# Two transformer layers on one core: last batch in token halves, mask rows inside the products, and new tables of times

## The reference

```python
x = x + LN(attn0(LN(x)))     # 16 heads of 16, biases, rope, causal softmax, Wo
x = x + LN(ffn0(LN(x)))      # int32 weights / 127, silu(gate) * up, hidden 768
x = x + LN(attn1(LN(x)))     # 16 heads of 64, 50 * tanh(sim / 50), causal softmax
x = x + LN(ffn1(LN(x)))      # below
xr = mu_r * x + (1 - mu_r) * x_prev        # x_prev: the token before
xk = mu_k * x + (1 - mu_k) * x_prev
out = sigmoid(xr @ Wr.T) * (square(relu(xk @ Wk.T)) @ Wv.T)
```

## Time and profile before

| | |
|---|---|
| runs | 1568.55, 1568.12, 1564.73 us; median 1568.12 |
| profiled execution | 1568.51 us, of which the profile's span is 1566.8 |
| busy | PE 1467.9 us, DVE 1143.9, ACT 808.6, POOL 812.9 |
| one batch of the first phase | about 81.3 us; of the second 101 us |
| mean granted PE clock | 0.973 |

### The profile page before, as it was taken

The page is one execution under the profiler, slowest core; times in us unless marked ns, Lnnn a source line. Parts: engine busy times, 40 slices in busy tenths (PEclk is TensorE's granted clock), DMA queues, the critical chain, the costliest instruction groups (busy, mean ns, idle before and its releaser), DMA issues.

```text
span 1566.8 us, 29295 instructions
## 1 busy us (share of the span) xinstructions
PE 1467.9 (94%) x10902; PEld 1063.1 (68%) x10902; DVE 1143.9 (73%) x1876; ACT 808.6 (52%) x1196; POOL 812.9 (52%) x1003
## 2 busy tenths in 40 slices
PE   3778999999999999999999999999999999999995
PEld 2545666666666767577777777777777777777774
DVE  5768787878887787865656868867678686785865
ACT  2334435353544444635565656665666566565641
POOL 3243535354444444335647567566666565665742
PEclk8888999999999999999999999999999999999997
DMA  6424242424242424120100010100100001000000
GB/s 158 68 42 68 42 82 42 82 41 81 41 81 41 67 41 78 59 68 21 41 28 1 1 41 1 41 1 1 40 0 28 12 0 40 0 0 28 1 28 14
DMA packets 47266, 60.82 MB, mean 39 GB/s; under 512 B 5296, under 2 KB 32848, under 8 KB 47184
## 3 DMA queue, kind: packets, MB, share of 16 engines
q1 hardware_dynamic: 46320, 59.03, 18.8%
q10 hardware_dynamic: 864, 0.66, 0.1%
HBM read 25.83 MB, written 8.39 MB: 22 GB/s over the span
## 4 chain that ended last, share of the span: by engine, by line
PE 86%; DVE 7%; ACT 3%; issue 2%; DMA 1%; POOL 1%; SPq 0%; POOLq 0%; DVEq 0%; ACTq 0%
PE psum L353 41%; PE psum L1708 9%; PE psum L1743 9%; PE psum L1759 6%; PE psum L997 5%; PE psum L1731 4%; PE psum L983 4%; PE psum L954 3%; DVE l_rowmax L823 2%; ACT l_probs L750 1%; PE psum L961 1%; PE psum L1017 1%; PE psum L1006 1%; DMA l_qT<-l_roped_hi 1%; ACT l_probs L1443 1%
## 5 line engine op out<-in xcount | busy, mean ns | idle before, releaser
L750 ACT ACTIVATE l_probs<-psum 128x512 f32<-128x512 f32 (+1 forms) x384 | 181.0, 524 | 212.1 <-PE psum L983 211.1
L823 DVE TENSOR_REDUCE l_rowmax<-psum 128x2 f32<-128x1024 f32 (+3 forms) x256 | 201.7, 818 | 56.5 <-PE psum L961 55.9
L1443 ACT ACTIVATE l_probs<-psum 128x1024 f32<-128x1024 f32 (+1 forms) x192 | 163.4, 878 | 135.1 <-PE psum L1708 119.7
L1527 DVE RECIPROCAL l_att<-psum 128x512 f32<-128x512 f32 x64 | 214.7, 3354 | 19.0 <-PE psum L1731 12.4
L1518 DVE TENSOR_TENSOR l_qk_lo<-psum,l_qk_hi 128x1024 fp32r<-128x1024 f32 x64 | 78.3, 1224 | 171.4 <-ACT l_qk_hi L1433 171.4
L232 POOL TENSOR_SCALAR_AFFINE_SELECT l_probs<-l_probs 128x256 f32<-128x256 f32 (+1 forms) x384 | 179.6, 499 | 0.0
L1449 ACT ACTIVATE l_probs<-l_probs 128x2048 f32<-128x2048 f32 (+1 forms) x128 | 161.6, 1270 | 1.3
L227 POOL TENSOR_TENSOR l_pool_holder<-expo 128x1 f32<-128x1 f32 x128 | 26.1, 204 | 257.1 <-ACT l_probs L1449 146.0
L1743 PE MATMUL psum<-l_probs,l_v 128*64 128x512 f32 (+3 forms) x1024 | 149.5, 434 | 0.0
L1743 PEld LDWEIGHTS psum<-l_probs,l_v 128*64 128x64 f32 x1024 | 72.2, 137 | 87.7 <-issue 76.9
L697 POOL TENSOR_TENSOR l_hT_lo<-l_gated,l_hT_hi 128x512 fp32r<-128x512 f32 x48 | 62.2, 1295 | 107.8 <-ACT l_hT_hi L764 107.8
(11 more groups left out here) (210 smaller groups left out, 4144.9 us busy)
## 6 DMA issues: line engine op xcount, KB each, us to landing
l_kT<-l_roped_hi SPq DMA_DIRECT2D x64, 128.0 KB, 4.0
l_qT<-l_roped_hi SPq DMA_DIRECT2D x64, 128.0 KB, 5.8
l_xin<-in_x SPq DMA_DIRECT2D x8, 512.0 KB, 4.0
l_kT<-l_roped_lo SPq DMA_DIRECT2D x32, 128.0 KB, 5.1
l_qT<-l_roped_lo SPq DMA_DIRECT2D x32, 128.0 KB, 6.3
l_x<-in_x SPq DMA_DIRECT2D x8, 512.0 KB, 4.0
x_mid<-l_x SPq DMA_DIRECT2D x8, 512.0 KB, 2.9
l_xin<-x_mid SPq DMA_DIRECT2D x8, 512.0 KB, 4.3
```

Source lines behind the costliest of these rows:

```text
L750: ring_s.free(nc.scalar.activation(probs[:, SLOT[p], e, c0:c1], ring_s.unit(*use)[:, 0:c1 - c0], ACT.Exp, scale=HD0 ** -0.5), *use)
L823: reduced = nc.vector.tensor_reduce(rowmax[:, a // 2, :, a % 2, t], ring_d.unit("max", a, k)[:, :, c0:c0 + (t + 1) * P], mybir.AxisListTyp ...
L1443: ring_s.free(nc.scalar.activation(probs[:, p % 2, :, c0:c1], ring_s.unit("score", p, u)[:, :, 0:c1 - c0], ACT.Tanh, scale=HD1 ** -0.5 / C ...
L1527: ring_d.free(nc.vector.reciprocal(att[p % 2][:], ring_d.unit("den", p)), "den", p)
```

## The change

**Mask rows.** `outT` holds, before its first use, a tile `marks` that POOL builds: 16 rows for `kT`, 16 for `qT`. Four DMAs of 256 KB lay them, repeated for the eight pairs, over rows 48 to 63 of both halves of `kT` and `qT`. Product by product the rows then add the large negative constant where the first 64 queries of a block meet the last 64 keys of the same block, in both passes. The `L961` product of h = 0 is therefore 64 columns wide rather than 128. The clearing of `kT` (DVE), of `qT` (POOL, two) and the eight small DMAs of the ones row are gone; PE waits for the four DMAs before its first `max`.

**Last batch.** For the last batch, the last pair's reciprocal, product, `att_hi` and `att_lo`, then `o` of that pair, the mix, `key`, `r`, the square and its split, the gate and the rest go in token halves.

**Tables.** All tables of times are replaced.

```diff
-        sp.wait_ge(consts, 6)
-        sp.wait_ge(k_cleared, 1)
-        for which in (0, 1):
-            for half in range(2):
...
-                sp.dma_start(kT[row:row + 1, 4 * half:4 * half + 4, 0:VONES].bitcast(F32),
-                             v0[0:1, :, 0:VONES]).then_inc(ones_placed, 16)
...
+        sp.wait_ge(consts, 17)
+        for dst, first in ((kT, 0), (qT, ROW0 - KMAX)):
+            for e in range(2):
+                sp.dma_start(dst[ROW0 * e + KMAX:ROW0 * e + ROW0, :, :].bitcast(F32),
+                             marks[first:first + ROW0 - KMAX, :].bitcast(F32).unsqueeze(1).to_broadcast([ROW0 - KMAX, PAIRS, T])).then_inc(rows_placed, 16)
...
-        nc.gpsimd.memset(qT[:, 0:PAIRS // 2, :].bitcast(F32), 0.0).then_inc(q_cleared, 1)
...
+        nc.gpsimd.memset(marks.bitcast(F32), 0.0).then_inc(consts, 1)
+        pool.wait_ge(consts, 14)
+        halves = marks.rearrange("p (t h c) -> p t h c", t=NT, h=2)
...
-        nc.vector.memset(kT[:].bitcast(F32), 0.0).then_inc(k_cleared, 1)
...
+            if a == 0 and k == 0 and not started(i):
+                pe.wait_ge(rows_placed, 64)
...
-                        last = nc.tensor.matmul(unit[:, e, c1 + ROW0 * h:c1 + P], rows_of[rows, h, :], later[rows, 0:P - ROW0 * h],
+                        last = nc.tensor.matmul(unit[:, e, c1 + ROW0 * h:c1 + ROW0 * h + ROW0], rows_of[rows, h, :], later[rows, 0:ROW0],
...
-        "score": {(0, 0): 4.26, (0, 1): 4.28, (0, 2): 5.77, (1, 0): 5.79, (1, 1): 5.81, (1, 2): 6.34, (2, 0): 12.11, (2, 1): 12.13, (2, 2): 12.6, (3, 0): 12.62, (3, 1): 13.5, (3, 2): 14.39, (4, 0): 15.33, (4, 1): 15.85, (4, 2): 15.87, (5, 0): 19.15, (5, 1): 19.29, (5, 2): 20.26, (6, 0): 24.42, (6, 1): 24.44, (6, 2): 24.96, (7, 0): 24.96, (7, 1): 24.98, (7, 2): 26.21},
...
+        def att_low(i, p):
+            if last_batch(i) and p == NP1 - 1:
+                for h, span in enumerate(SPANS):
+                    pool.wait_ge(attT_hi.sem, attT_hi.at(i, p + 1 + h))
...
+            if last_batch(i) and p == NP1 - 1:
+                half = lambda span: nc.vector.tensor_tensor(att[p % 2][:, span], att[p % 2][:, span], ring_d.unit("pv", p)[:, span], ALU.mult)
+                dve.wait_ge(rden_ready, 1)
+                ring_d.filled(dve, i, "pv", p)
+                half(SPANS[0]).then_inc(att_first, 1)
+                ring_d.free(nc.vector.reciprocal(att[p % 2][:, SPANS[1]], ring_d.unit("den", p)[:, SPANS[1]]), "den", p)
...
+        def key_half(h):
+            x = [part[:, :, SPANS[h]] for part in mixk]
+            for c in range(NC):
+                last = width_major(nc, ring_s.unit("key")[:, h, SPANS[c]], x, wrkv[:2], slice(D + c * P, D + (c + 1) * P), NC)
+            return last
...
+            if last_batch(i):
+                pe.wait_ge(mix_split.sem, mix_split.at(i, 1))
+                key_half(0).then_inc(key_first, 1)
+                return
             pe.wait_ge(mix_split.sem, mix_split.at(i, 2 * NC - 1))
```

More of the change, by code:

```diff
@@ new lines, in phase2 @@
+        "r_out": {(): 43.01},
+        "key_b": {(): 42.37},
+        "key": {(): 42.33},
+        "key_out_b": {(): 42.99},
+        "key_out": {(): 42.97},
+        "square_b": {(): 44.23},
+        "square": {(): 44.21},
+        "kact_hi_b": {(): 44.45},
+        "kact_hi": {(): 44.43},
+        "kact_lo_b": {(): 45.31},
+        "kact_lo": {(): 45.29},
+        "out_b": {(): 53.96},
+        "out": {(): 47.96},
+        "gate_b": {(): 48.66},
+        "gate": {(): 45.97},
+        "x4_stats_b": {(): 49.02},
@@ L1465, in mixed, with sigmoid, receptance_b @@
                 act.wait_ge(mix_ready.sem, mix_ready.at(i, 2 * c + k + 1))
[L1466 removed]
+                part, whole = mixed_part(i, c, k)
+                nc.scalar.activation(part(dst[0]), whole, ACT.Copy).then_inc(mix_hi.sem, 1)
+        def sigmoid(i, h):
+            return nc.scalar.activation(sig_r[:, HALVES[h], :].rearrange("p t d -> p (t d)"), ring_s.unit("r")[:, h, :], ACT.Tanh, scale=0.5)
+        def receptance_b(i):
+            if last_batch(i):
+                ring_s.filled(act, i, "r")
+                ring_s.free(sigmoid(i, 1), "r")
         def receptance(i):
+            if last_batch(i):
+                act.wait_ge(r_first, 1)
+                sigmoid(i, 0).then_inc(sig_first, 1)
+                return
             ring_s.filled(act, i, "r")
@@ L1784, in x3_T_b, with tokens, products_b, tiles @@
                 ring_s.fill(x3_T_tiles(i, HALVES[1]), "x3_T")
-        def tokens(name, x, cols, ready, count):
+        def tokens(name, x, cols, ready, count, first):
             def products(i):
                 ring_s.claim(pe, i, name)
-                pe.wait_ge(ready.sem, ready.at(i, count))
+                if last_batch(i):
+                    pe.wait_ge(ready.sem, ready.at(i, first))
+                else:
+                    pe.wait_ge(ready.sem, ready.at(i, count))
                 weights.split(pe, i, 10)
-                for t in range(NT):
+                last = tiles(HALVES[0] if last_batch(i) else slice(0, NT))
+                if last_batch(i):
+                    last.then_inc(r_first if name == "r" else out_first, 1)
+                else:
+                    ring_s.fill(last, name)
+            def products_b(i):
+                if last_batch(i):
+                    pe.wait_ge(ready.sem, ready.at(i, 2 * first))
+                    ring_s.fill(tiles(HALVES[1]), name)
+            def tiles(part):
+                for t in range(part.start, part.stop):
                     last = token_major(nc, ring_s.unit(name)[:, t // 2, (t % 2) * D:(t % 2 + 1) * D], x, wrkv[:2], t, cols, NC)
-                    if name == "out" and last_batch(i) and t == NT // 2 - 1:
-                        last.then_inc(out_first, 1)
-                ring_s.fill(last, name)
-            return products
+                return last
+            return products, products_b
         def end_heat(i, n):
```

459 lines of the change are left out of this document (272 added, 187 removed).

## The result

The changed kernel takes 1576.0 us, the median of 14 runs (1573.7 to 1581.8), against 1568.5 for the one before (1564.7 to 1573.7). The ratio is 1.0048, 95% interval 1.0035 to 1.0061: slower by 7.5 us, where 12 us less was forecast. The profiled execution took 1580.1 us, 4 above its median; its span is 1578.4, 11.6 over the one before. So the differences found between the two traces add up to 11.6 and overstate the difference of the medians.

A forecast was written before the change was run, and what follows sets the result against it. PE was taken to bound the kernel, busy 1467.9 of 1566.8 us. The terms −6 + 4.4 − 3.8 − 4.8 − 2 = −12.2 us gave 1556.0 us from the median of 1568.1, range 1546 to 1568.

The forecast's parts named there:

- the passage: Between the first and second phase: taken at nothing (±1 us).
- the clock: First phase's half-clock stretches: each costs 1.75 us, six go or stay with the order; no term in the sum.
- Mask products: Narrower mask products save 7.7 us of PE columns; a fifth given back to waits on DVE: −6 us (0 to −9.6).
- rival C: Everything at its better end, including full clock in the last batch: −23.7 us, 1544.4; chance 0.15.
- the six stretches could double: First phase's half-clock stretches double instead of going: 10 us more, ending near 1566, within rival A's chance.
- rival A: Only half arrives: mask saving falls into first-phase waits, mode changes were hiding PSUM waits; −2.6 us, 1565.5; chance 0.2.
- Start: Program start: four new DMAs keep the queue busy, so placing DMAs and first maxima come later: +4.4 us (0 to +10).
- Order in the second phase: Five fewer mode changes a batch at 0.2 us, less 0.6 a batch for ACT: −4.8 us (0 to −8).
- Rival B: Second phase: four score units in a row wait for ACT, up to 2.5 us a batch; 1581; chance 0.1 for slower.
- Order in the first phase: 47 mode changes a batch become 44, while waits behind exponentials and maxima move: −2 us (+4 to −5).
- Last batch: Token halves let the second phase's last chain start sooner, partly at full clock: −3.8 us (−2 to −6).
- three cases: Last batch, 18 products ahead of `key`: 4.3, 5.5 or 7.3 us, settling which clock they run at.

The follow-up runs named there:

- masks_only: The kernel before with only the mask rows and the 64-column first mask product, all tables as before: 1567.2 us, ratio 0.9990.
- best_parts: The kernel before, old tables, with mask rows, six extra unread products per first-phase batch, last batch in halves and its second-half statistics moved: 1560.2 us, ratio 0.9938.
- wide_mask: The changed kernel with the first mask product widened again to 128 columns: 1575.8 us, ratio 1.0045.
- heats_in_stall: The changed kernel with six more unread products per first-phase batch, at PE's two waits for ACT and DVE: 1561.6 us, ratio 0.9956.
- heats_before: The kernel before with six more unread products per first-phase batch, at the same waits for ACT and DVE: 1563.0 us, ratio 0.9952.
- p1_table_old: The changed kernel with the old tables of the first phase and of the start put back: 1574.2 us, ratio 1.0039.

## Why the prediction was wrong

Two steps failed by most: the passage, which the sum took at nothing, and the clock, for which it had no term. Neither of the two things that I had named as what would make me wrong by most happened: a batch of the second phase is not longer, and the start is not late.

**The passage between the phases.** The prediction took it "at nothing (±1)", without a reason. It is +6.6 us by the account. 2.57 us of it are one wait, and the move that takes it away brought 3.5. I had not asked what each piece there waits for. Another 2.1 us are smaller waits, which were not taken apart, and 1.9 are busy time at a lower clock.

**Mask products.** The mechanism held, and so, nearly, did the price of a product. Eight of them take 0.13 us, from start to start, where 0.12 was forecast and 0.18 was measured before:

```profile
260.75 0.29 PE L960 MATMUL psum<-l_later,l_rows_of 64*128 64x64 bf16 x8
260.88 0.53 PE L980 MATMUL psum<-l_qT,l_kT 64*128 64x128 f32 x4
```

That is 0.05 for two blocks (0.06 where a change of mode follows), 6.4 to 7.7 us in all, where I had 7.7. By the Trainium skill ("TensorE: Matmul & The Clock Gate", Back-to-back issue gap) the estimate of the gross saving was 7.9 us. What failed is the share that I gave back to the waits. At full clock 0.3 us of a batch (`masks_only`) to 0.52 (`best_parts`) remain of 0.8 to 0.96: 2.4 to 4.2 us over eight batches and not 6. And with the clock as it is, `masks_only` is 1.6 us below the kernel before, which is within the noise.

**The clock** stood in the prediction only as a part of rival C and as a remark that the six stretches could double. I put that near 1566 and counted it to rival A. They did double, in each batch that was looked at, and the sum had no term for it. `wide_mask` shows that the narrow products did it, at an unchanged time: the clock gave back what they saved. `heats_in_stall` against `heats_before` shows the size: 14.4 us are won by holding the clock in the changed kernel and 5.9 in the one before, so 7 to 9 us of the change's loss are the clock.

**Start.** +4.4 was forecast and nothing came. The queue was filled for even longer than worked out: the last load of before was issued at 12.60, and after it is this, which landed 11.6 us later, at 31.0.

```profile
19.35 0.43 SPq L624 DMA_DIRECT2D l_xin<-in_x  x1
```

The placing DMAs were issued from 21.71 on, as before, and ran beside that load at first. But they moved faster, and the first maxima were at 36.5 again. The step that failed is the rate, which I took for a property of these copies: the earlier trace rows has 100 GB/s in the window from 25 to 37, in which the copies had ended before the window did. From 31 to 34 both kernels move these copies alone, at 125 GB/s before and at 208 after:

```profile
31.00:34.00 3.00, 0.00 (x0) 0.00 (x0) 0.00 (x0) 0.00 (x0) 0.00 (x0) 0.50 1.10 125
```

```profile
31.00:34.00 3.00, 0.00 (x0) 0.00 (x0) 0.00 (x0) 0.00 (x0) 0.00 (x0) 0.50 0.94 208
```

**Order in the second phase.** −4.8 was forecast, −1.7 came (0.28 us a batch over six). Five changes of mode fewer at 0.2 us would be 1.0 a batch. (At the third projection there were three changes and there is one now; PE went there from 64-row products to whole-array ones twice, and not three times.) The price per change was read rightly from the earlier trace rows; what was wrong is that it could be saved. For two of the five this is shown: they cost 0.12 and not 0.4, since a pause was waiting behind them. What became of the other three was not taken apart. Rival B, which had PE wait for ACT by up to 2.5 us a batch, has the mechanism and too large a size: the batch is shorter all the same.

**Order in the first phase.** −2 was forecast. With everything else of the change in place the new tables cost 1.9 us (`p1_table_old` against the changed kernel), which is within the noise of the two.

**Last batch.** −3.8 was forecast, −3.1 came, with the 18 products ahead of `key` still mostly at half clock:

```profile
1546.65 1.08 PE L1896 MATMUL psum<-ident,l_xn 128*128 128x128 f32 x4 [2.73 <-DVE l_xn L345]
1549.26 1.12 PE L1896 MATMUL psum<-ident,l_xn 128*128 128x128 f32 x4 [1.52 <-DVE l_xn L345]
1551.06 6.91 PE L360 MATMUL psum<-l_wrkv_hi 128*128 128x512 f32 x18 [0.69 <-ACT l_xs L1525]
```

The wait before the transposes is halved, as worked out, and the group takes 6.91 us where 7.27 were before. So of the three cases that the prediction named for this group (4.3, 5.5 and 7.3 us) it was the half-clock one.

## What to carry to other kernels

When a stream of matmuls has stalls that another engine sets, work taken away beside them can lengthen the time at the lower granted clock, and that can cost as much as was saved. Read the granted clock of one iteration before and after, and try a few products without a reader in the stall: here six a batch brought 6 us to one kernel and 14 to the other. Compare two orders only with the clock held in both.

A pause that a piece in between had covered shows in no row as idle time. Before counting such a piece's price as a gain, look when the buffer behind it comes free. And where a whole order is replaced, the passage between two phases deserves the same reading as the loops: one wait there cost 2.6 us, and the whole passage 6.6, more than the mask products were to bring in all eight batches.

## What the runs showed of the hardware that was not expected

Between the start and the last few us of these traces, the lower clock comes in stretches of 3.4, 6.8 or 10.2 us (the earlier trace rows and the windows above). Whether a batch has none, a short or a double one differs between batches of one execution that issue the same instructions (79.80, 81.00 and 81.60 us in `masks_only`). It also differs between runs: of the 53 of the kernel before, 38 lie about 1568.3 us at a mean clock of 0.974 and 14 about 1573.8 us at 0.969 (medians).

The same copies from SBUF to SBUF moved at 125 GB/s in one program and at 208 in the other, in the same 3 us. What differs is that in the faster one they queued behind loads and the broadcasts of the mask rows. DVE's work is not the reason: before, the rate was 127 from 25 to 29 us with DVE busy for 3.15 us and 124 from 29 to 33 with DVE idle. And `masks_only`, in which DVE worked there as before (2.99 us from 25 to 29) and the loads were queued as after, moved 194 GB/s from 28.5 to 31 us, behind the landing of its last load. How the queue's filling does it stays open.
